# One layer stack on one core: the first feed-forward's experts weighted by ScalarE and added by POOL, and two loads moved behind the first rows

## The reference

```python
x = x + mamba(layernorm(x))      # in_proj, conv, silu; 16 states per channel, scan over time
x = x + ffn(layernorm(x))        # 8 experts, top 2 by router
x = x + attn(layernorm(x))
x = x + ffn(layernorm(x))        # the same weights

# scan:  new = exp(A * delta) * state + delta * B_t * h_t ;  y = sum_n new * C_t + D * h_t
# ffn:   w_e = weight of expert e if among the token's top 2, else 0
#        out += w_e * ((x @ w_up[e]) * silu(x @ w_gate[e])) @ w_down[e]
```

## Time and profile before

| engine | busy us | share | instructions |
|---|---|---|---|
| PE (TensorE) | 588.0 | 97% | 4572 |
| DVE (VectorE) | 498.4 | 82% | 1079 |
| ACT (ScalarE) | 400.5 | 66% | 852 |
| POOL (GpSimd) | 383.9 | 63% | 360 |

### The profile page before, as it was taken

How to read it: one execution, slowest core, us unless ns; L and a number is a source line. 1 busy time by engine, 2 the same in 40 slices (tenths; PEclk the granted TensorE clock), 3 DMA queues, 4 the chain that set the end, 5 groups by cost and what they waited for, 6 DMA issues and landing times.

```text
span 609.3 us, 13178 instructions
## 1 busy us (share of the span) xinstructions
PE 588.0 (97%) x4572; PEld 551.3 (90%) x4572; DVE 498.4 (82%) x1079; ACT 400.5 (66%) x852; POOL 383.9 (63%) x360
## 2 busy tenths in 40 slices
PE   8879999899999999999999999999999999999997
PEld 7633788489999999999999999999999999999997
DVE  5598889878998999999989999899999995454443
ACT  7976675668668786868587858777676732525340
POOL 1278385479886997689878979599757863000000
PEclk9999999989999999999999999999999999999999
DMA  8933213202230212222210231012222000000000
GB/s 281 282 150 130 93 70 115 96 8 86 79 137 18 75 74 83 82 81 72 83 70 24 96 129 69 22 73 79 82 78 77 2 15 12 12 1 15 1 23 9
DMA packets 18466, 45.43 MB, mean 75 GB/s; under 512 B 2847, under 2 KB 13664, under 8 KB 14178
## 3 DMA queue, kind: packets, MB, share of 16 engines
q1 hardware_dynamic: 18402, 44.61, 21.0%
HBM read 40.15 MB, written 1.31 MB: 68 GB/s over the span
## 4 chain that ended last, share of the span: by engine, by line
PE 82%; ACT 6%; DVE 4%; issue 3%; DMA 3%; POOL 1%; SPq 1%; DVEq 0%; ACTq 0%
PE ps L1438 24%; PE ps L1208 15%; PE ps L1209 14%; PE ps L1210 14%; PE ps L1374 3%; ACT dA L831 3%; PE ps L1487 2%; DVE st L1086 2%; DMA at_uv<-uv_w 1%; PE ps L1478 1%; PE ps L1203 1%; PE ps L1499 1%; PE ps L1293 1%; PE ps L1326 1%; POOL st L644 1%
## 5 line engine op out<-in xcount | busy, mean ns | idle before, releaser
L644 POOL TENSOR_TENSOR st<-st,rows_ring 128x512 f32<-128x512 f32 x128 | 164.4, 1289 | 62.1 <-DVE st L1086 58.5
L1438 PE MATMUL ps<-down,inner_ring 128*128 128x128 f32 (+1 forms) x1408 | 174.4, 275 | 0.7 <-DVE X L1171 0.7
L883 ACT ACTIVATE sg<-ps 128x512 f32<-128x512 f32 x176 | 104.7, 596 | 101.9 <-PE ps L1210 82.3
L1438 PEld LDWEIGHTS ps<-down,inner_ring 128*128 128x128 f32 (+1 forms) x1408 | 167.2, 191 | 3.7 <-issue 1.9
L1086 DVE TENSOR_TENSOR_SCAN st<-dA,ps 128x512 f32<-128x512 f32 x128 | 154.8, 1212 | 2.8 <-ACT dA L831 0.3
L1157 DVE TENSOR_TENSOR inner_ring<-sg,ps 128x512 f32<-128x512 f32 x176 | 118.9, 679 | 44.0 <-ACT sg L883 23.5
L657 POOL TENSOR_TENSOR yacc<-yacc,st 128x512 f32<-128x512 f32 x96 | 125.0, 1302 | 5.1
L831 ACT ACTIVATE dA<-delta,A 128x255 f32<-128x255 f32 x256 | 104.8, 495 | 0.2
L1208 PE MATMUL ps<-xhi,up_hi 128*128 128x256 f32 x352 | 102.6, 291 | 0.0
L1209 PE MATMUL ps<-xlo,up_hi 128*128 128x256 f32 x352 | 99.8, 283 | 0.0
L1210 PE MATMUL ps<-xhi,up_lo 128*128 128x256 f32 x352 | 99.8, 283 | 0.0
(11 more groups left out here) (152 smaller groups left out, 865.4 us busy)
## 6 DMA issues: line engine op xcount, KB each, us to landing
rows_ring<-bc SPq DMA_DIRECT2D x31, 1024.0 KB, 4.8
moved_rows<-inner_ring SPq DMA_DIRECT2D x96, 32.0 KB, 1.9
inner_ring<-gate_w SPq DMA_DIRECT2D x1, 1408.0 KB, 8.0
inner_ring<-up_w SPq DMA_DIRECT2D x1, 1408.0 KB, 10.6
down<-down_w SPq DMA_DIRECT2D x2, 512.0 KB, 10.4
out<-X SPq DMA_DIRECT2D x8, 128.0 KB, 1.8
X<-x SPq DMA_DIRECT2D x1, 768.0 KB, 7.3
rows_ring<-bc SPq DMA_DIRECT2D x1, 768.0 KB, 5.1
```

The source lines that it names most:

```text
L644: nc.gpsimd.tensor_tensor(st[:, i % NST], st[:, i % NST], row, ALU.mult).then_inc(s["m_p"], 1)
L883: nc.scalar.activation(sg[:, k % 2], two(bank_of(q, 2 * j)), ACT.Silu).then_inc(s["f_sg"], 1)
L1438: ins = nc.tensor.matmul(bank_of(q, 2 * NP + e)[:, c * H:(c + 1) * H], act_in, down[0:rows, e, n, :], start=n == 0, stop=n == NB - 1)
```

## The change

Three things. The load of the down weights moves on SP from directly behind the setup loads to a place between the second and the third block of rows of sequence 0 (the third block's own time moves from 1602 to 1620, which changes nothing else in the order). The load of sequences 2 to 7 moves from ahead of the first rows to behind the fourth block. And pass 0's `combine` leaves VectorE: ScalarE multiplies expert e's two halves out of PSUM by the weight into a scratch tile (at_base and at_q, which the attention uses later), two instructions of 128x128 (semaphore f_sc); POOL adds the tile to X, one instruction of 128x256. The bank is now free once ScalarE has read it. The ScalarE steps take the places of the old combine steps in the order, the POOL steps stand 0.6 us later. Passes 1 to 15 stay as they are.

```diff
+NSCALE = 1
-    "rows": [1590, 1596, 1602, 2951, 4561, ...
+    "rows": [1590, 1596, 1620, 2951, 4561, ...
-    "load_down": [87],
+    "load_down": [1614],
-    "load_x": [1435],
+    "load_x": [2957],
-    "combine": [8427, 8482, 8855, 8915, 9237, 9745, 9800, 10246, 14064, ...
+    "combine": [8487, 8542, 8915, 8975, 9297, 9805, 9860, 10306, 14064, ...
+    "scale": [8427, 8482, 8855, 8915, 9237, 9745, 9800, 10246],
...
+        scaled = [at_base, at_q]
...
+            if k >= 2 * NP and q < NSCALE:
+                return s["f_sc"], NE * q + k - 2 * NP + 1
             if k >= 2 * NP:
                 return s["f_x"], COMB * q + NC * (k - 2 * NP + 1)
...
+            def combine(arg):          # POOL
+                q, e = arg
+                if q >= NSCALE:
+                    return
+                u, _ = QUEUE[q]
+                pool.wait_ge(s["f_sc"], NE * q + e + 1)
+                if e:
+                    pool.wait_ge(s["f_x"], COMB * q + NC * e)
+                part = scaled[e % 2][:].rearrange("p (c h) -> p c h", c=NC)
+                nc.gpsimd.tensor_tensor(X[:, u], X[:, u], part, ALU.add).then_inc(s["f_x"], NC)
...
+            def scale(arg):            # ScalarE
+                q, e = arg
+                act.wait_ge(s["f_dn"], NE * q + e + 1)
+                if e == 0:
+                    act.wait_ge(s["r_w"], q + 1)
+                if e > 1:
+                    act.wait_ge(s["f_x"], COMB * q + NC * (e - 1))
+                for c in range(NC):
+                    ins = nc.scalar.activation(scaled[e % 2][:, c * H:(c + 1) * H], bank_of(q, 2 * NP + e)[:, c * H:(c + 1) * H],
+                                               ACT.Copy, scale=wts[:, q % 2, c, e:e + 1])
+                ins.then_inc(s["f_sc"], 1)
...
             def combine(arg):          # VectorE
                 q, e = arg
+                if q < NSCALE:
+                    return
```

More of the change, by code:

```diff
@@ L62 @@
  n_var n_rstd n_neg n_xc n_xm n_xt n_hi n_lo r_lg r_sum r_nh r_mr r_th r_is r_w2 r_w
- f_G f_U f_sg f_in f_dn f_x
+ f_G f_U f_sg f_in f_dn f_x f_sc
  a_pb a_b a_qk a_pu a_u a_pv a_v a_sc a_rl a_sq a_av a_ua a_wo a_bs a_x
@@ L80 @@
     "diag1": [829],
-    "rows": [1590, 1596, 1602, 2951, 4561, 4567, 5181, 7039, 8615, 9534, 10606, 12685, 14140, 15618, 17008, 19612,
+    "rows": [1590, 1596, 1620, 2951, 4561, 4567, 5181, 7039, 8615, 9534, 10606, 12685, 14140, 15618, 17008, 19612,
         20963, 22119, 23508, 25790, 27414, 28809, 29914, 32751, 33875, 35043, 36405, 38786, 40262, 41353, 42873,
@@ L255 @@
     "lo_rows": [9580],
-    "combine": [8427, 8482, 8855, 8915, 9237, 9745, 9800, 10246, 14064, 14131, 14417, 14688, 14743, 14843, 15122,
+    "combine": [8487, 8542, 8915, 8975, 9297, 9805, 9860, 10306, 14064, 14131, 14417, 14688, 14743, 14843, 15122,
         15247, 17156, 17297, 17353, 17731, 17793, 18064, 18119, 18231, 20806, 21077, 21201, 21378, 21433, 21557,
@@ L293, in arguments @@
         return itertools.product(range(2 * S), range(NP))
+    if name == "scale":
+        return itertools.product(range(NSCALE), range(NE))
     if name in ("down", "combine"):
@@ L668, in _ @@
                           "m_mul2": conv_product(2), "m_add2": conv_sum(2), "m_mul3": conv_product(3), "m_add3": conv_sum(3), "mulC": mulC,
-                          "sum": sum_states, "m_gate": m_gate})
+                          "sum": sum_states, "m_gate": m_gate, "combine": combine})
         @block.scalar
@@ L931, in _ @@
                           "m_y0": m_y0, "decay": decay, "n_nb": n_nb, "n_norm": n_norm,
-                          "n_hi": n_hi, "r_th": r_th, "silu": silu, "a_b": a_b, "a_qk": a_qk, "a_u": a_u,
+                          "n_hi": n_hi, "r_th": r_th, "silu": silu, "scale": scale, "a_b": a_b, "a_qk": a_qk, "a_u": a_u,
                           "a_v": a_v, "a_rl": a_rl, "a_sq": a_sq})
```

## The result

The changed kernel takes 603.92 us (median of four runs, 602.45 to 605.28) where the kernel before, on the same chip, takes 611.16 (610.47 to 612.3). The ratio is 0.9879, with a 95% interval of 0.9852 to 0.9907: faster by 7.2 us. The forecast was 5.9 us and 605.4, with 603.8 as the lower end; the measured time stands at that end. By the ratio the gain is 7.4 us, which is 603.9 on the 611.3 from which the forecast was made. The direction and the mechanism came as written; the size was taken too small, by 1.3 us by the medians and 1.5 by the ratio.

What follows compares the result with a forecast made beforehand. Sequence 0's state loop, full on VectorE and POOL, was taken to start late because VectorE waited for rows behind a late bc. -6.1 for the loads plus 0.2 for the experts gave -5.9: 605.4 us as the median, range 603.8 to 608.3.

Steps and rivals of the forecast that it cites:

- The bound and the wait: Sequence 0's state loop starts late: VectorE's product of state 2 waits for rows, held up by bc's late issue on SP.
- rival b: ScalarE ends last before scan 1, so earlier rows bring nothing: 611.5 to 612.3; 8% with other ends near the old time.
- Part 1: The two moved loads: bc goes out earlier, state 2 starts sooner on VectorE, 6.1 us gained.
- the time at which VectorE is free for state 2: VectorE, start of sequence 0's state loop: free at 23.6, so state 2 starts there instead of at 29.51.
- The term for bc: SP, before the first rows: bc issued at 14.05 and landed at 18.0, 19.0 as the late end.
- the late add: POOL's add 7 delays the product of state 15 and TensorE's last sum of sequence 1 by 0.2 us (0 to 0.95).
- Does the loop follow?: Sequence 0's loop and all after move as a whole; POOL, first only 4.4 us earlier, catches up two or three states later.
- Part 2: Pass 0's experts moved from VectorE to ScalarE and POOL: the relief gives nothing, and the move costs 0.2 us.
- (a): Third block of rows comes late, mild form: 1.3 us lost, up to half the gain, 606.7 to 608.5; 13%.
- (c): Third block of rows starved, landing at 45: 7.7 us lost, slower at 613.1; 5% with whatever else is slower.
- (d): ScalarE's pairs and POOL's adds dearer: late by 0.95 + 0.5 at most, 606.2 to 606.9; within the forecast's 74%.

Runs made afterwards that it cites:

- loads-only: The kernel before with only the two loads (down weights, sequences 2 to 7) moved, VectorE keeping its weighted additions: 603.82 us, ratio 0.9882.
- experts-only: The changed kernel with both loads back in their old places, pass 0's experts still weighted by ScalarE and added by POOL: 610.45 us, ratio 1.0002.
- pairs-in-four: The changed kernel with each of ScalarE's pairs of 128x128 multiplications done as four instructions of 128x64: 604.16 us, ratio 0.9908.
- no-zeros: The changed kernel without the matmuls by zeros between the late sums of sequences 0 and 1: 602.78 us, ratio 0.9884.
- holes filled: The changed kernel with seven useless matmuls before TensorE's wait for sequence 1's gate and five before pass 1's norm: 602.52 us, ratio 0.9873.

## Why the prediction's mechanism was right, and where its size was off

**The bound and the wait: right.** I set the chain of waits aside for the idle row, and it was the rows that ended last, not ScalarE. Had ScalarE been the end (rival b), loads-only would have shown no gain.

**Part 1, the size: this is the step that failed.** "I take 6.1" was 6.68, above even the 6.6 that I had as the most. The term that was mis-sized is the time at which VectorE is free for state 2: I took 23.6, and it was 22.83. The 23.6 came from an execution in which ScalarE had waited 1.08 us for two loads; no other trace has more than 0.34 us of that, experts-only with the old loads included. I had tied these waits to the down weights and took 0.2 us for them. The term for bc was too slow as well: I gave it 3.95 us because the chain of waits shows 3.33 for a transfer into an empty queue, while the profile's list of DMA issues gives a median of 1.5 for the eight of them, and that row was the odd one. It landed in 1.5 to 2.5 us in the kernels that move the down weights behind the first rows. So the rows, which I had at 22.9, were there at 22.56, and VectorE's own list set the start.

The 6.68 itself moves from execution to execution. In the traces with the old loads state 2 stands at 29.51 and 29.54, though xe ran at 13.57 in one and 14.26 in the other. In the changed kernel, loads-only, pairs-in-four, no-zeros, and those with the holes filled or the down weights behind the fourth block it follows xe by 8.6 to 8.7 us and lies between 22.25 and 22.89, which is 6.6 to 7.3 us earlier and 6.9 on the mean. That leaves 0.3 us to the 7.2 of the medians, which is less than their spread.

**A term that I had not seen.** The slow bc of sequence 1 cost 0.43 us in the trace of before (the gate of sequence 0 at 61.63, 61.20 in experts-only). It stood in the earlier trace rows, and I used its length without asking whom it holds up. With it the terms of the two traces add up: 6.68 + 0.43 = 7.11, against 7.08 between the last sums, with the late add at zero. It is chance, not the change's doing, and it says nothing of the medians: a wait of over 1.7 us for these rows stands in 3 of the 14 traces, one of them the kernel with the down weights behind the fourth block.

**Does the loop follow?** Yes: 6.68 at state 2, 6.67 at state 8 and 7.1 from 54 us on, above the 5.5 to 6.5 that I gave. POOL caught up: its next product came at 26.19, and by 30.60 it waited 0.65 us for VectorE again.

**Part 2: right that it gives nothing, its cost too high.** Forecast 0.2 (0 to 0.95), measured 0. The form that the trace lacked, 128x128 out of PSUM, has a mean of 360 ns, below the nearest rows. I counted 0.70 us for each of three pairs; each took 0.50 from its neighbours. That is shown by the two equal stretches of loads-only and experts-only, and the margin by pairs-in-four. My reason, that TensorE is full there, holds for these kernels only: without its matmuls by zeros it waits 2.43 us for POOL, and whether VectorE's relief would count then was not tried.

**The rivals.** (a) and (c) were about the third block. Moving the down weights further back brought nothing, moving them one place forward cost 4.7 us in the trace: the price per microsecond was right and the margin at the chosen place was there. (d) holds only for slower pairs, and its top was added up wrong: 611.3 - 6.1 + 0.95 + 0.5 is 606.7, not 606.9.

**Not forecast: the clock.** It moves single executions by 1.5 us, as much as the error of the forecast. The rows for it were in the trace of before, and the prediction has no word on it. It does not explain the 7.2 us: with mean clocks of 0.997 on both sides the spans differ by 7.1, and the slowest execution of the changed kernel (605.28) is 5.2 us below the fastest of the kernel before on that chip (610.47).

What stays open: why bc of sequence 1 takes 1.5 us in most traces and 3.3 to 3.7 in two; why xe runs at 13.5 in some executions and 14.3 in others; and what decides whether the clock falls, since four of the twelve traces with the holes open show no fall behind them. The second hole is not needed for it: in experts-only the clock is at half from about 118.5, behind the first hole (to 117.99) and ahead of the second (to 122.76).

## What to carry to other kernels

Read a load's place by two costs: the time for which the issuing queue stands in it, and the bytes that it puts ahead of whatever is issued behind it; both fall on the next small transfer that someone waits for, and mending the first alone leaves the second. Work out, block by block, when each is first read: here one place in the order was worth 4.7 us in the trace and the next one nothing. Before work is moved off a busy engine, look whether another engine is full in that stretch: sixteen instructions less on VectorE were worth 0. And a time read from a single execution can hold a wait that the next one does not have: look for it in a second trace before it becomes a term of a sum.

## What the runs showed of the hardware

- TensorE's granted clock fell to half speed for 3 to 4 us around or behind the holes of 1.7 and 1.4 us in seven of the eleven traces that have these holes and the matmuls by zeros, at a cost of 0.4 to 1.6 us in the rest of the span. With twelve matmuls of no use in the holes, all four executions had a mean clock of 1.00. Without the zeros, with a wait of 2.43 us ahead of the holes, the half speed began behind that wait and lasted over 6 us.
- The product of delta and h, which reads two tiles of SBUF on VectorE, took 0.69 us in the kernel before (at 111.74) and 1.13 in the changed one (at 103.52), where it starts while POOL works on its products of states 13 and 14:

```profile
103.52 1.13 DVE L1084 TENSOR_TENSOR ps<-delta,h 128x512 f32<-128x512 f32 x1
```
```profile
101.58 2.50 POOL L664 TENSOR_TENSOR st<-st,rows_ring 128x512 f32<-128x512 f32 x2
```

  It ends 0.57 us, nearly its own length, after POOL does. So it does in two other traces whose starts differ: in experts-only it starts at 110.19 and takes 1.12, in pairs-in-four it starts at 102.93 and takes 1.73, and both end 0.56 us behind POOL's products. The Trainium skill ("SBUF — State Buffer", SBUF: two separate sides) says that a VectorE instruction with two SBUF inputs and a GpSimd instruction that reads SBUF take an exclusive lock in turn; these three cases agree, though no run was made to test it. It cost nothing, for the product of state 15 waited for the late add.
- SP stood 8.29, 6.75 and 3.74 us in the same three issues of the down weights in the kernel before, the changed one and the one with them right behind bc; the order fits what was queued ahead, which no run isolates.
